# Loading the input and the adjacency a second time with rows and columns exchanged, and taking the gated layer's scalars as extra columns of a product

## The reference, cut to what matters

```python
x = _layernorm(x + L0(x, adj, ...))   # attention, 4 heads, masked by adj
x = _layernorm(x + L1(x, adj, ...))   # gated layer, 4 heads
x = _layernorm(x + L2(x, adj, ...))   # 8 heads, cosine threshold and softmax
x = _layernorm(x + L3(x, adj, ...))   # attention as L0
# L1, for each head:
Wh = h @ W.T + bW
e = Wh @ attn
A_mat = tanh(where(adj, e @ Wh.T, 0))
hp = relu(A_mat @ Wh)                  # heads side by side: cat
ha = cat @ A_w.T;  hf = h @ fc_w.T
coeff = sigmoid(hf @ g1_w.T + ha @ g2_w.T + gbias)
out = hf * coeff + ha * (1 - coeff)
```

## Time and profile before

| | us |
|---|---|
| median of 3 runs | 2617.25 |
| lowest, highest | 2616.52, 2620.95 |
| the profiled execution, its own time | 2622.45 |
| its span from the first to the last instruction | 2620.5 |

### The profile page before, as it was taken

One profiled execution on the slowest core, in us unless ns is written; L12 is line 12 of the kernel. 1 busy time (PEld: TensorE's weight loads), 2 busy tenths in 40 slices (PEclk: granted clock), 3 DMA queues, 4 the chain that ended last, 5 costly groups with the idle time before them and its releaser, 6 DMA issues.

```text
span 2620.5 us, 63291 instructions
## 1 busy us (share of the span) xinstructions
PE 2558.4 (98%) x22097; PEld 2291.7 (87%) x22097; DVE 2007.6 (77%) x6629; ACT 1409.9 (54%) x3925; POOL 918.1 (35%) x988
## 2 busy tenths in 40 slices
PE   7999999999999999999999999999999999999996
PEld 7888888898888898888898888898888898888884
DVE  4477878877878877878877877877877777877875
ACT  2355555655555655555655555655655655654653
POOL 3233333343333343333343333343333343333331
PEclk8999999999999999999999999999999999999998
DMA  4000000000000000000000000000000000000000
GB/s 136 7 1 12 11 11 1 10 10 10 10 10 0 10 10 10 10 10 0 10 10 10 10 10 0 10 10 10 10 10 0 10 10 10 10 10 1 11 7 9
DMA packets 44490, 29.90 MB, mean 11 GB/s; under 512 B 21264, under 2 KB 44048, under 8 KB 44432
## 3 DMA queue, kind: packets, MB, share of 16 engines
q1 hardware_dynamic: 44432, 29.13, 3.8%
HBM read 20.73 MB, written 8.39 MB: 11 GB/s over the span
## 4 chain that ended last, share of the span: by engine, by line
PE 84%; ACT 4%; DVE 3%; issue 1%; POOL 0%; ACTq 0%; DVEq 0%; POOLq 0%
PE bank L474 21%; PE bank L476 19%; PE bank L475 19%; ACT arena L606 4%; PE bank L1451 4%; PE bank L531 3%; PE bank L540 3%; PE bank L463 3%; PE bank L1441 3%; PE bank L551 3%; PE bank L1431 2%; PE bank L1462 2%; DVE arena L690 1%; PE bank L1261 1%; DVE arena L647 0%
## 5 line engine op out<-in xcount | busy, mean ns | idle before, releaser
L405 POOL TENSOR_SCALAR l_ve<-l_mv 128x2 f32<-128x2 f32 x128 | 29.0, 226 | 1031.2 <-DVE l_mv L390 1030.9
L474 PE MATMUL bank<-arena_r 128*128 128x256 f32 x1024 | 303.3, 296 | 0.2
L1605 ACT ACTIVATE b<-b,s_sh 128x256 f32<-128x256 f32 x496 | 246.7, 502 | 88.4 <-DVE s_sh L647 88.3
L476 PE MATMUL bank<-arena_r 128*128 128x256 f32 x1024 | 289.0, 282 | 0.0
L475 PE MATMUL bank<-arena_r 128*128 128x256 f32 x1024 | 289.0, 282 | 0.0
L1885 POOL TENSOR_TENSOR arena_r<-a,arena_r 128x512 fp32r<-128x512 f32 x128 | 166.2, 1299 | 329.6 <-ACT arena_r L1541 329.5
L1880 POOL TENSOR_TENSOR arena_r<-a,arena_r 128x512 fp32r<-128x512 f32 x128 | 166.2, 1299 | 171.6 <-ACT arena_r L1547 171.5
L474 PEld LDWEIGHTS bank<-arena_r 128*128 128x128 f32 x1024 | 194.6, 190 | 22.8 <-issue 22.2
L1775 DVE SCALAR_TENSOR_TENSOR b<-bank,b 128x256 f32<-128x256 f32 x496 | 184.8, 421 | 30.9 <-ACT b L1605 25.7
L475 PEld LDWEIGHTS bank<-arena_r 128*128 128x128 f32 x1024 | 195.2, 191 | 0.0
L476 PEld LDWEIGHTS bank<-arena_r 128*128 128x128 f32 x1024 | 194.8, 190 | 0.0
(11 more groups left out here) (304 smaller groups left out, 9060.5 us busy)
## 6 DMA issues: line engine op xcount, KB each, us to landing
x_in<-in_x SPq DMA_DIRECT2D x32, 256.0 KB, 2.8
out<-x SPq DMA_DIRECT2D x32, 256.0 KB, 2.1
adj_a<-in_adj SPq DMA_DIRECT2D x32, 64.0 KB, 2.5
adj_b<-in_adj SPq DMA_DIRECT2D x32, 64.0 KB, 1.9
a<-in_L_gnn_W SPq DMA_DIRECT2D x4, 256.0 KB, 3.4
b<-in_L_gnn_A_w SPq DMA_DIRECT2D x1, 1024.0 KB, 7.8
arena<-in_L_gnn_attn SPq DMA_DIRECT2D x4, 256.0 KB, 7.1
g_b_wh<-in_L_gnn_bW SPq DMA_DIRECT2D x1, 512.0 KB, 8.4
```

The source lines that it names most:

```text
L474: pe.matmul(out, w[0], x[0], start=first, stop=False)
L476: return pe.matmul(out, w[1], x[0], start=False, stop=last)
L1605: last = act.activation(R.e[h // QUAD][:, n, it, :], R.e[h // QUAD][:, n, it, :], ACT.Exp, bias=S.sh[:, it, h:h + 1], scale=-1.0, accum_ou ...
```

## The change

1. The launch gets two more inputs, `x_t` and `adj_t`: `x` and `adj` with the last two axes exchanged. They are made on the host ahead of the launch, as contiguous arrays.
2. `load_a` also loads `x_t` into `x_t_in`, and `a_x_t` of ScalarE and VectorE reads it from there. TensorE's `a_x_t` is gone.
3. `load_t` loads `adj_t` as bytes, and GpSimd's `g_adj` writes `G.adj_t` from it. `g_adj_t` of TensorE and VectorE is gone.
4. The weights of `G.c` are four more columns beside those of head 0 (`G.w_tc`, 260 columns). `g_wh_0` writes two banks, and VectorE adds the scalars' bias. `g_c` and `g_c_t` are gone.
5. In setup `A_w`'s transposes and split come after the products with `attn`, and the loads are sorted by that.
6. The three tables are written anew for every engine; the loop's body begins at another stage.

The two orders of TensorE in the loop, and the code (the other engines' tables are left out):

```diff
-        ("b_values_1", 2), ("g_ha_2_0", 1), ("g_ha_1_1", 1), ("b_out", 2), ("g_ha_2_1", 1), ("g_ha_3_1", 1),
-        ("g_ha_3_0", 1), ("g_hf", 1), ("g_ha_t", 1), ("g_gate_x", 1), ("d_x_t", 2), ("g_gate", 1), ("a_x_t", 0),
+        ("g_wh_1", 1), ("b_unit_t", 2), ("g_z_1", 1), ("g_s_0", 1), ("b_scores_0", 2), ("g_z_2", 1), ("g_s_1", 1),
+        ("g_wh_2", 1), ("b_cos_0", 2), ("g_z_3", 1), ("b_transpose_0", 2), ("b_transpose_1", 2), ("g_p_0", 1),
+        ("b_transpose_2", 2), ("b_transpose_3", 2), ("g_s_2", 1), ("b_values_0", 2), ("g_wh_3", 1), ("b_scores_1", 2),
+        ("g_p_1", 1), ("g_s_3", 1), ("g_ha_0_0", 1), ("b_cos_1", 2), ("g_ha_1_0", 1), ("g_p_2", 1),
+        ("b_transpose_4", 2), ("b_transpose_5", 2), ("g_ha_0_1", 1), ("b_transpose_6", 2), ("b_transpose_7", 2),
+        ("g_ha_2_0", 1), ("g_p_3", 1), ("b_values_1", 2), ("g_ha_1_1", 1), ("b_out", 2), ("g_ha_3_0", 1),
+        ("g_ha_2_1", 1), ("g_ha_3_1", 1), ("g_hf", 1), ("g_ha_t", 1), ("g_gate_x", 1), ("d_x_t", 2), ("g_gate", 1),
         ("d_q", 2), ("d_k", 2), ("d_v", 2), ("d_scores_0", 2), ("d_scores_1", 2), ("a_k", 0), ("a_v", 0), ("a_q", 0),
         ("d_probs_0", 2), ("d_probs_1", 2), ("a_scores_0", 0), ("d_probs_2", 2), ("d_probs_3", 2), ("a_scores_1", 0),
         ("d_values_0", 2), ("d_values_1", 2), ("b_x_t", 1), ("a_probs_0", 0), ("a_probs_1", 0), ("a_probs_2", 0),
-        ("a_probs_3", 0), ("a_values_0", 0), ("a_values_1", 0), ("d_out", 2), ("a_out", 0), ("b_m", 1), ("b_k", 1),
-        ("b_q", 1), ("g_x_t", 0), ("g_adj_t", 0), ("b_sem", 1), ("g_wh_0", 0), ("g_c", 0), ("g_z_0", 0),
-        ("g_wh_1", 0), ("g_c_t", 0), ("b_unit_t", 1), ("g_z_1", 0), ("b_scores_0", 1), ("g_wh_2", 0), ("g_s_0", 0),
-        ("g_z_2", 0), ("b_cos_0", 1), ("g_s_1", 0), ("g_z_3", 0), ("b_transpose_0", 1), ("b_transpose_1", 1),
-        ("g_p_0", 0), ("b_transpose_2", 1), ("b_transpose_3", 1), ("g_s_2", 0), ("b_values_0", 1), ("g_wh_3", 0),
-        ("b_scores_1", 1), ("g_p_1", 0), ("g_s_3", 0), ("g_ha_0_0", 0), ("b_cos_1", 1), ("g_ha_1_0", 0), ("g_p_2", 0),
-        ("b_transpose_4", 1), ("g_ha_0_1", 0), ("b_transpose_5", 1), ("b_transpose_6", 1), ("b_transpose_7", 1),
-        ("g_p_3", 0),
+        ("a_probs_3", 0), ("a_values_0", 0), ("a_values_1", 0), ("d_out", 2), ("a_out", 0), ("b_m", 1), ("b_q", 1),
+        ("b_k", 1), ("g_x_t", 0), ("b_sem", 1), ("g_wh_0", 0), ("g_z_0", 0),
...
@@ -1169,20 +1166,29 @@
         def _(sp):
             def load_a(g):
                 if later(g):
+                    sp.wait_ge(A.x_t_sb.sem, A.x_t_sb.all(g - 1))
+                apart(sp)
+                sp.dma_start(x_t_in[:, :, :], d["x_t"][g].rearrange("(t p) n -> p t n", p=P)).then_inc(x_t_loaded.sem, 16)
+                if later(g):
                     sp.wait_ge(A.x_bias.sem, A.x_bias.all(g - 1))
-                if later(g):
-                    sp.wait_ge(A.x_t_psum.sem, A.x_t_psum.all(g - 1))
                 apart(sp)
                 sp.dma_start(x_in[:, :, :], d["x"][g].rearrange("(t p) n -> p t n", p=P)).then_inc(x_loaded.sem, 16)
                 if later(g):
-                    sp.wait_ge(G.adj_bf_ready.sem, G.adj_bf_ready.all(g - 1))
+                    sp.wait_ge(A.mask.sem, A.mask.all(g - 1))
                 apart(sp)
                 sp.dma_start(adj_a[:, :, :], d["adj"][g].rearrange("(t p) n -> p t n", p=P)).then_inc(adj_a_loaded.sem, 16)
+
+            def load_t(g):
+                if later(g):
+                    sp.wait_ge(G.adj_sb.sem, G.adj_sb.all(g - 1))
+                apart(sp)
+                sp.dma_start(adj_t_in[:, :, :], d["adj_t"][g].rearrange("(t p) n -> p t n", p=P)).then_inc(adj_t_loaded.sem, 16)
...
+            load_t(2)
             with sp.Fori(2, GRAPHS - 1) as t:
                 store(t - 2)
                 load_a(t + 1)
                 load_b(t)
+                load_t(t + 1)
...
-
-            def g_adj_t(g):
-                pe.wait_ge(G.adj_bf_ready.sem, G.adj_bf_ready.at(g))
-                adj_bank = BA[3][:, 0:NODES].bitcast(BF16)
-                for mt in range(T):
-                    for nt in range(T):
-                        last = pe.transpose(adj_bank[:, mt * NODES + nt * P:mt * NODES + (nt + 1) * P],
-                                            G.adj_bf[:, nt, mt * P:(mt + 1) * P], C.ident_bf[:, :])
-                last.then_inc(G.adj_psum.sem, 1)
...
-                pe_node_major(pe, BA[1], G.xt, G.w_t[h]).then_inc(G.wh_psum.sem, 1)
-
-            def g_c(g):
-                pe.wait_ge(G.x_t_sb.sem, G.x_t_sb.at(g))
-                for kc in range(T):
-                    for half in range(2):
-                        last = pe.matmul(BA[2][0:2 * HG, 0:NODES], G.w_c_rows[:, kc, :], G.xt[half][:, kc, :],
-                                         start=(kc == 0 and half == 0), stop=(kc == T - 1 and half == 1))
-                last.then_inc(G.c_psum.sem, 1)
-
-            def g_c_t(g):
-                pe.wait_ge(G.c_sb.sem, G.c_sb.at(g, 1))
-                for it in range(T):
-                    last = pe.transpose(BA[2][:, NODES + it * P:NODES + (it + 1) * P],
-                                        G.c_all[:, it * P:(it + 1) * P], C.ident[:, :])
-                last.then_inc(G.c_psum.sem, 1)
+                    pe.wait_ge(G.c_sb.sem, G.c_sb.at(g))
+                if h == 0:
+                    for it in range(T):
+                        for kc in range(T):
+                            last = pe_product(pe, BA[1 + it][:, 0:DIM + HG],
+                                              part(G.xt, slice(None), kc, slice(it * P, (it + 1) * P)),
+                                              part(G.w_tc, slice(None), kc), kc == 0, kc == T - 1)
+                    last.then_inc(G.wh_psum.sem, 1)
+                else:
+                    pe_node_major(pe, BA[1], G.xt, G.w_t[h]).then_inc(G.wh_psum.sem, 1)
...
 
             def g_a(g, h):
                 act.wait_ge(G.a_f.sem, G.a_f.at(g, h + 1))
+                if h >= 2:
+                    act.wait_ge(G.p_psum.sem, G.p_psum.at(g, h - 1))
                 act.activation(G.am[h % 2][0], G.th[:, h % 2, :, :], ACT.Copy).then_inc(G.a_hi.sem, 1)
...
-                if stage.startswith("a_"):
+                if stage == "a_x_t":
+                    act.wait_ge(x_t_loaded.sem, x_t_loaded.all(g))
+                    if later(g):
+                        act.wait_ge(G.p_psum.sem, G.p_psum.all(g - 1))
+                    act.activation(A.xt[0], x_t_in[:, :, :], ACT.Copy).then_inc(A.x_t_hi.sem, 1)
...
@@ -1568,11 +1562,6 @@
                     g_z(g, int(stage[4:]))
                 elif stage.startswith("g_s_"):
                     g_s(g, int(stage[4:]))
-                elif stage == "g_c":
-                    act.wait_ge(G.c_psum.sem, G.c_psum.at(g, 1))
-                    if later(g):
-                        act.wait_ge(G.ha_psum.sem, G.ha_psum.all(g - 1))
-                    act.activation(G.c_rows, BA[2][0:2 * HG, 0:NODES], ACT.Identity, bias=G.b_c[:, :]).then_inc(G.c_sb.sem, 1)
                 elif stage.startswith("g_a_"):
                     g_a(g, int(stage[4:]))
                 elif stage.startswith("g_p_"):
...
                 dve.wait_ge(G.wh_psum.sem, G.wh_psum.at(g, h + 1))
                 if h >= 2:
                     dve.wait_ge(G.wh_sb.sem, G.wh_sb.at(g, h - 1))
+                elif h == 0 and later(g):
+                    dve.wait_ge(G.tanh.sem, G.tanh.all(g - 1))
                 for it in range(T):
-                    last = dve.tensor_tensor(G.whf[:, h % 2, it, :], BA[1][:, it * DIM:(it + 1) * DIM],
-                                             G.b_wh[:, h * DIM:(h + 1) * DIM], ALU.add)
+                    src = BA[1 + it][:, 0:DIM] if h == 0 else BA[1][:, it * DIM:(it + 1) * DIM]
+                    last = dve.tensor_tensor(G.whf[:, h % 2, it, :], src, G.b_wh[:, h * DIM:(h + 1) * DIM], ALU.add)
                 last.then_inc(G.wh_f.sem, 1)
+                if h == 0:
+                    for it in range(T):
+                        last = dve.tensor_tensor(G.c[:, it, :], BA[1 + it][:, DIM:DIM + HG], G.b_c[:, :], ALU.add)
+                    last.then_inc(G.c_sb.sem, 1)
 
             def g_z(g, h):
...
 
             def slot_a(stage, g):
-                if stage.startswith("a_"):
+                if stage == "a_x_t":
+                    dve.wait_ge(A.x_t_hi.sem, A.x_t_hi.at(g))
+                    dve.tensor_tensor(A.xt[1], x_t_in[:, :, :], A.xt[0].bitcast(F32), ALU.subtract).then_inc(A.x_t_sb.sem, 1)
+                elif stage.startswith("a_"):
                     a_slot(stage[2:], g)
-                elif stage == "g_adj_t":
-                    if later(g):
-                        dve.wait_ge(G.a_f.sem, G.a_f.all(g - 1))
-                    dve.wait_ge(G.adj_psum.sem, G.adj_psum.at(g))
-                    dve.tensor_copy(G.adj_t[:, :, :], BA[3][:, 0:NODES].bitcast(BF16).rearrange("p (a n) -> p a n", n=NODES))\
-                        .then_inc(G.adj_sb.sem, 1)
...
```

(27 more changed lines are left out.)

## The result

The changed kernel takes 2654.33 us (median of 4 runs, 2650.59 to 2657.18) where the kernel before takes 2619.1 in the same comparison: a ratio of 1.0132, 95% interval 1.012 to 1.0144. It is 35 us slower; 2591 us, 26 us faster, had been forecast, and a pass of 79.5 us is over the 78 that the prediction had named as a sign of being wrong.

What follows compares the result with a forecast made beforehand. TensorE, busy 98% of the span, was taken as the bound, partly filling chains through ScalarE and VectorE. 0.44 + 0.30 - 0.04 = 0.70 us a graph, 22.4 us, plus 3.5 in setup, gave 2591 us against the median; range 2582 to 2600.

Steps and rivals of the forecast that it cites:

- The other engines: Work on ScalarE, VectorE, GpSimd and loads, and TensorE's reordered steps from g_z_1 to b_out: costed at nothing.
- Rival (3): Reordered stretch: new waits of 0.7 us a pass take all the gain, 2613 to 2621 us; chance 0.06.
- The rule on the shared port: VectorE with two SBUF inputs and GpSimd lock each other out; a_x_t's subtraction might pay 0.32 us, 10 us in sum.
- `g_adj_t` and `g_c_t`: TensorE steps of 0.26 and 0.22 us; removal gives nothing, as g_wh_0 and g_z_1 wait for VectorE anyway.
- `g_c`: TensorE step ahead of g_z_0: 0.46 us a graph come back, 0.44 after the wider products.
- 260 columns: The 12 products of g_wh_0, widened from 256, stay in the fast form and cost 0.02 us a graph.
- rival (4): Products of g_wh_0 leave the fast form, costing 3.8 us a graph: 2713 us; chance 0.03.
- `a_x_t`: TensorE transposes between g_gate and d_q: 0.30 of 0.44 us a graph come back, bounds 0 and 0.44.
- Handovers: Handovers between engines made tighter by the new sequences: 0.04 us a graph lost.
- The setup's order: Before the loop: products with attn start near 11 us instead of 16.76; worth 3.5 us, bounds 0 and 8.

Runs made afterwards that it cites:

- e10: Changed kernel with d_mask, d_norm_out, d_stats and d_rstd moved in the order tables, VectorE's body not shifted: 2651.41 us, pass 79.46 us.
- e11: Changed kernel, VectorE's body 39 instructions further on, d_norm_out put behind g_z_0 with d_stats and d_rstd earlier, d_mask unmoved: 2612.06 us, pass 77.95 us.
- e1: Changed kernel with 39 more idle instructions at the head of VectorE's program, so its loop body lies further on: 2641.44 us, pass 78.99 us.
- e7: Changed kernel, VectorE's body 39 instructions further on, d_mask moved, unread transposes on TensorE at three removed steps' places: 2631.62 us, pass 78.62 us.
- e8: All the changed code under the order tables of the kernel before, removed steps struck, GpSimd's g_adj of two graphs later: 2613.46 us, pass 78.03 us.
- e4: Kernel before with 46 more idle instructions at the head of VectorE's program: 2660.09 us, ratio 1.0136 to 1.0170, pass 79.87 us.

## Why the prediction was wrong, by its own steps

**The step that failed** is "The other engines", at two places. It cost the new order of VectorE at nothing, because VectorE has 1550.63 us of 1957.87, and it took the new stretch from `g_z_1` to `b_out` for the same TensorE steps in another order. A share of busy time says nothing of the 2 us between masks and cuts, where the old order left VectorE idle for 0.56 us (1425.81 to 1426.37) and the new one adds `d_norm_out`. VectorE in the kernel before, `d_norm_out` in its old place behind `g_z_0`, and `g_p_1` and `g_a_3` between the masks and the cuts:

```profile
1402.87 0.73 DVE L397 TENSOR_SCALAR x<-x,l_mv,l_rs 128x256 f32<-128x256 f32 x2
...
1426.37 0.69 DVE L1692 SCALAR_TENSOR_TENSOR arena_r<-bank,arena_r 128x512 fp32r<-128x512 f32 x1 [0.56 <-ACT arena_r L1551]
1427.09 0.69 DVE L1687 TENSOR_TENSOR a<-a,g_adj_t 128x512 f32<-128x512 f32 x1
```

The prediction saw that `d_norm_out` was moved behind the masks, and weighed this for the loads alone; it followed `a_x_t`'s subtraction through VectorE's list, but not this instruction. By the rows of before it adds 0.73 us there. It took 1.08 in the changed kernel: its second half took 0.76 us for 0.41, beside GpSimd's `d_mask`, which starts with it. And the change begins the body at another stage; what the jump costs there was not asked. The jump was in the trace of before, at 0.28 us; that it could cost 3 us no row showed. What the runs showed in place of nothing: at this point the jump alone costs 1.51 us a pass (79.46 - 77.95, e10 and e11), `d_norm_out` alone 1.04 (78.99 - 77.95, e1 and e11), and both together 1.56.

Rival (3) named the stretch ("New waits of 0.7 us a pass in the reordered stretch") and under half of the size, which was 1.63, and put 0.06 on it; it ended at no change. Nothing among the rivals was slower for this reason. Within the stretch the wait was to be looked for at `g_p_1`, `b_cos_1` and `g_ha_2_0`; it came at the transposes behind `b_cos_1`, through VectorE's cuts. The rule on the shared port was weighed at the wrong instruction: `a_x_t`'s subtraction takes 0.68 us in the changed kernel. VectorE's half of `d_x_t`, the `d_v` copy, the subtraction and the first mask there:

```profile
1374.27 0.69 DVE L637 TENSOR_TENSOR b_r<-bank,b_r 128x512 fp32r<-128x512 f32 x1 [0.58 <-ACT b_r L582]
...
1379.75 0.69 DVE L665 COPY b<-bank 128x512 f32<-128x512 f32 x1 [0.16 <-PE bank L471]
1380.36 0.68 DVE L1693 TENSOR_TENSOR arena_r<-x_t_in,arena_r 128x512 fp32r<-128x512 f32 x1
1380.96 0.42 DVE L642 CUSTOM_DVE_ANT_0 b<-bank,l_add 128x256 f32<-128x256 f32 x1
```

Where the same rule did bite was `g_a_3`, longer by 1.10 us in e1.

**The other steps, in e11, where nothing else stands in the way.**

`g_adj_t` and `g_c_t`, forecast at nothing: right. `g_x_t` to `g_wh_0` is 2.13 us for 2.14, the last of `g_z_0` to `g_z_1` 2.21 for 2.21, and e7 shows the places empty. The waits are there, but no bracket tells of them. In the changed kernel's timeline of TensorE:

```profile
1404.69 0.66 PE L458 MATMUL bank<-ident,a 128*128 128x128 f32 x4
...
1406.49 0.28 PE L471 MATMUL bank<-s_w_s_hi,b32r 128*128 128x256 f32 x1
1406.82 0.39 PE L469 MATMUL bank<-g_w_tc_hi,arena_r 128*128 128x260 f32 x1
1407.05 0.28 PE L470 MATMUL bank<-g_w_tc_lo,arena_r 128*128 128x260 f32 x1
1407.17 0.28 PE L471 MATMUL bank<-g_w_tc_hi,arena_r 128*128 128x260 f32 x1
```

The last product of `b_sem` is issued at 1406.49, the first of `g_wh_0` 0.33 us later instead of 0.12. A product lasts 0.28 us in this view, so all but 0.05 us of the gap lies inside it and counts as busy: busy time can grow while work is taken out.

`g_c`, forecast at 0.44: 0.37. 260 columns keep the fast form, as forecast (1407.05 to 1407.17, 0.12 us a product; rival (4) is out). But the first product behind the wait takes 0.23 us to the next, where it took 0.16 (1397.73 to 1397.89 in the kernel before). This is the 0.07 that is missing.

`a_x_t`, forecast at 0.30: 0.22 up to `d_q`, of which 0.05 go again before `g_x_t`. `d_q` starts 0.36 us behind the last product of `g_gate` and not 0.12. In the changed kernel:

```profile
1374.75 0.28 PE L471 MATMUL bank<-g_w_g_hi,arena_r 128*128 128x256 f32 x1
1375.11 0.36 PE L469 MATMUL bank<-b_r,arena_r 128*128 128x256 f32 x1
```

VectorE's half of `d_x_t` ends at 1374.27 + 0.69 = 1374.96, 0.15 us ahead, where 0.1 had been taken for the handover. The rest of the gap is no loss: `g_gate` starts 0.36 us behind `d_x_t` (1373.36 - 1373.00), where it took 0.50 (1364.17 - 1363.67), so TensorE is there earlier and waits. The masks begin 7.96 us after `d_x_t` (1380.96 - 1373.00) in the changed kernel, with 7.85 forecast and 8.15 before.

Handovers, forecast at -0.04: -0.12 from `g_z_1` to `g_ha_t`, and -0.05 from `g_z_0` to `g_z_1`. e8 loses about the same at both under the old tables (37.20 us for 37.09, 3.53 for 3.47), so it is not the new sequences that cost it; what does was not taken apart. Together 0.38 a pass for 0.70: even without the two causes the time is 2612 us (e11) and not 2591.

The setup's order came out as forecast:

```profile
6.97 3.34 PE L458 MATMUL bank<-ident,a 128*128 128x128 f32 x16 [6.97 <-DMA a<-in_L_gnn_W]
10.15 7.17 PE L958 MATMUL bank<-a,arena 128*128 128x256 f32 x32
```

The products with `attn` start at 10.15 (forecast: near 11; before: 16.76). What it is worth can't be told: the start of `d_out` of graph 2 came at 369.94 and 365.41 us in the two profiles of the old code (before, e4), and between 362.2 and 369.5 in those of the new. The time from `d_out` of graph 27 to that of graph 31, 284.1 and 283.5 us in the old code, is 286.8 to 289.7 in all profiles of the new, under the old last table too (e8). Those 3 to 6 us were not taken apart and stay open.

## What to carry to other kernels

Where a change rewrites the orders of all engines, follow every engine's list across the stretch that ends last, and price what newly stands between two ends of a chain; the mean load of the engine is no cover. Look at each engine's jump back as at an instruction, with what is queued behind it: its cost hangs on where the body happens to lie, so that any edit ahead of the loop can make or break it (39 us here, for 46 idle instructions). And when one cause is removed and little comes back, look for the next one behind it at the same place before giving up the theory: here 35 us of loss became a gain of 9 (e11, 2612.06 for 2621.43 us) only after the second.

## What the runs showed of the hardware that was not expected

VectorE's jump back takes 0.28 to 0.34 us or 2.8 to 3.1 us, by the place of a body of 290 instructions (293 in the kernel before) alone; with the long form come five transfers of 8 KB of instructions a pass, and a shift by 128 instructions changes nothing. TensorE's body, 1403 instructions a pass, jumps in 0.27 us in the changed kernel, and there no other instruction packets than these five a pass move from 440 us to `d_out` of graph 27. The profile shows the stall as "issue" where nothing else was due (e4), and under the name of whichever engine signalled last where something was (ScalarE, in the changed kernel).

Of two instructions of VectorE and GpSimd that meet, the later one pays, even by a start of 0.04 us (1.79 for 0.69 on VectorE) or 0.16 us (1.67 for 1.28 on GpSimd). It doesn't always pay for the whole rest: in the changed kernel `g_mix` starts 0.08 us behind GpSimd's making of a mask from bytes, and takes 1.08 us for 0.69, while that instruction is shown for 1.93. VectorE and GpSimd there:

```profile
1376.59 1.08 DVE L1725 SCALAR_TENSOR_TENSOR a<-a 128x512 f32<-128x512 f32 x1 [0.77 <-ACT a L1584]
```

```profile
1376.51 1.93 POOL L728 TENSOR_SCALAR l_add<-adj_a 128x512 bf16<-128x512 uint8 x1
```
